# The edge pass of a graph attention layer: own row added ahead of TensorE, bias and sigmoid taken from PSUM

## What is computed

```
for m in range(3):                        # attention
    h = x @ Ws[m]; s = h @ att_src[m]; d = h @ att_dst[m]
    e = leaky(s[src] + d[dst])            # edges and one self loop per node
    w = exp(e - segment_max(e)[dst])
    alpha = w / segment_sum(w, dst)[dst]
    x = x + sigmoid(segment_sum(alpha * h[src], dst) + bias[m])
...                                       # then three message layers of MLP type
```

## Time and profile before

| what | value |
|---|---|
| timed, median of 3 runs | 13333.38 us (13315.89 to 13337.69) |
| profiled execution, its own time | 13224.56 us |
| its span, first to last instruction | 13222.7 us |
| mean granted TensorE clock | 0.73 of full speed |
| edge pass 1 (m = 0) | 2643 to 3433 us, 49 rounds |
| edge pass 2 (m = 1) | 4056 to 4834 us, 49 rounds |
| edge pass 3 (m = 2) | 5465 to 6470 us, 49 rounds |

### The profile page before, as it was taken

The page is one execution under the profiler, slowest core; times in us unless marked ns, Lnnn a source line. Parts: engine busy times, 40 slices in busy tenths (PEclk is TensorE's granted clock), DMA queues, the critical chain, the costliest instruction groups (busy, mean ns, idle before and its releaser), DMA issues.

```text
span 13222.7 us, 165920 instructions
## 1 busy us (share of the span) xinstructions
PE 6805.4 (51%) x35028; PEld 5020.9 (38%) x35028; DVE 5117.0 (39%) x21443; ACT 3990.4 (30%) x8589; POOL 6568.4 (50%) x6253
## 2 busy tenths in 40 slices
PE   6777200077205730355322247777445888444888
PEld 3333100066205630355322235555333555333666
DVE  6777422366315641455322234443112333111444
ACT  7999300033102310233200024443112444111443
POOL 3444566544664566444677743233665333665000
PEclk9999655588657865677555568888556999555999
DMA  6777666644574457533233345565445777444998
GB/s 219 264 262 264 220 237 237 227 126 125 194 261 158 129 174 257 179 119 121 67 45 45 45 117 201 202 202 189 60 58 128 240 234 236 83 58 88 272 268 256
DMA packets 2128228, 2270.53 MB, mean 172 GB/s; under 512 B 234960, under 2 KB 1554869, under 8 KB 2121824
## 3 DMA queue, kind: packets, MB, share of 16 engines
q1 hardware_dynamic: 1798266, 1848.65, 42.2%
q0 software_dynamic: 321440, 418.37, 15.0%
q10 hardware_dynamic: 8390, 2.21, 0.1%
HBM read 1067.73 MB, written 1222.73 MB: 173 GB/s over the span
## 4 chain that ended last, share of the span: by engine, by line
DMA 14%; issue 11%; PE 8%; another core or an unknown queue 5%; POOL 4%; DVE 4%; SPq 3%; POOLq 1%; DVEq 0%; ACT 0%; ACTq 0%
DMA agg_d<-dO,fOI 10%; PE ps L1290 5%; DMA bXd<-agg_d 3%; POOL bO L810 2%; POOL agg_d L801 2%; PE ps L1267 2%; SPq L595 1%; DVE aO L1809 1%; PE ps L1277 1%; DVE bXd L1782 1%; PE ps L1265 1%; SPq L593 1%; DVE eE L1803 1%; SPq L602 0%
## 5 line engine op out<-in xcount | busy, mean ns | idle before, releaser
L862 POOL DMA_INDIRECT bXs<-x_d,fGI x784 | 798.6, 1019 | 1494.8 <-DMA x_d<-aH 1279.9
L801 POOL DMA_INDIRECT agg_d<-dO,fOI x784 | 1212.1, 1546 | 530.9 <-ACT dO L982 296.9
L1290 PE MATMUL ps<-W,aT 128*128 128x128 f32 x9408 | 1206.4, 291 | 22.8 <-ACT aS L999 15.6
L1277 PE MATMUL ps<-aS,W1X 128*128 128x512 f32 x2352 | 1207.4, 594 | 5.4 <-DMA eET<-eaT_d 5.2
L1290 PEld LDWEIGHTS ps<-W,aT 128*128 128x128 f32 x9408 | 1181.7, 208 | 39.7 <-ACT aS L999 25.9
L982 ACT COPY dO<-ps 128x128 f32<-128x128 f32 (+1 forms) x1176 | 318.2, 271 | 2733.7 <-DMA agg_d<-dO,fOI 1526.6
L1817 DVE TENSOR_TENSOR aH<-ps,B 128x512 f32<-128x512 f32 x588 | 406.4, 692 | 1848.1 <-PE ps L1290 1151.8
L1246 PE MATMUL ps<-bO,bNE 128*128 128x128 f32 x1568 | 568.9, 473 | 1021.5 <-ACT dO L982 1010.0
L1005 ACT ACTIVATE aT<-ps,BNT,BNS 128x512 f32<-128x512 f32 x1176 | 882.4, 774 | 609.2 <-PE ps L1278 574.7
L747 POOL DMA_INDIRECT bXs<-x_d,bGI x784 | 784.3, 1000 | 392.8 <-issue 247.7
L1246 PEld LDWEIGHTS ps<-bO,bNE 128*128 128x128 f32 x1568 | 382.5, 305 | 1198.1 <-issue 912.2
(11 more groups left out here) (260 smaller groups left out, 17793.7 us busy)
## 6 DMA issues: line engine op xcount, KB each, us to landing
agg_d<-zeros SPq DMA_DIRECT2D x788, 256.0 KB
bXd<-agg_d SPq DMA_DIRECT2D x784, 256.0 KB
agg_d<-zeros SPq DMA_DIRECT2D x394, 290.0 KB
bXd<-agg_d SPq DMA_DIRECT2D x392, 290.0 KB
x_d<-aO SPq DMA_DIRECT2D x392, 256.0 KB, 2.1
yg_d<-aYG SPq DMA_DIRECT2D x196, 512.0 KB, 3.1
aX<-yg_d SPq DMA_DIRECT2D x392, 256.0 KB, 4.2
x_d<-aH SPq DMA_DIRECT2D x392, 256.0 KB
```

The costliest lines, as they stand in the source:

```text
L801: pool.indirect_dma_start(agg_d[m][u % 2], bass.IndirectOffsetOnAxis(ap=index, axis=0), dO[:, u, 0:AW[m]], None, bounds_check=agg_last, oo ...
L862: pool.indirect_dma_start(fX[:, s, u, 0:C], None, gin_in[m], bass.IndirectOffsetOnAxis(ap=fGI[:, s, u:u + 1], axis=0), bounds_check=n_last ...
L1277: pe.matmul(z, W1X[:, m, h * P:(h + 1) * P], eHT[:, k, :], start=True, stop=False)
L1290: mm = pe.matmul(ps[6 + k][:, j * P:(j + 1) * P], eZ[:, k, h, j * P:(j + 1) * P], W2[:, m, h, :], start=(h == 0), stop=(h == 1))
```

## The change

**Own rows ahead of TensorE.** `diagonals` becomes `own_rows`: ScalarE scales the eight own rows of `pXd` instead of the identity, so it now waits for the loads (`l_in`) and for `p_xw`. A new VectorE step `joined(i+1)` at the end of its round multiplies the source rows by their weight and adds the scaled own rows in place (8 instructions, inputs `bXs` and `bSW`, both in SBUF). AG then has one matmul per tile, not two, and waits for `p_xw`. The masks are the comparison alone.

**Bias row, sigmoid from PSUM.** The denominators are stored to a DRAM tensor `den_d` once per pass and loaded, one row per round, into partition 32 of `pIN`; the bias stands in partition 32 of the carry operand `pCW`. The RW matmul so adds bias times denominator. The 8 VectorE steps L1675 are gone; ScalarE takes 8 sigmoids of one tile each straight from PSUM with 1/denominator as scale, in place of two of four tiles.

**Order.** VectorE does the scan right after the masks and before the dots. ScalarE does the sigmoids of i-1 before the own rows of i+1. The first loads of a pass wait for the end of the softmax section.

```diff
+                sp.wait_ge(z_v, ZV * (m + 1))
+                sp.dma_start(den_d.rearrange("r (h n) -> (r h) n", h=2), slU).then_inc(s_den, 16)
                 load_rows_of(0, 0)
+                sp.wait_ge(s_den, 16 * (m + 1))
...
-                def diagonals(i, s, m=m):
+                def own_rows(i, s, rr, n, m=m):
                     act.wait_ge(p_fe, m * R + i + 1)
+                    act.wait_ge(l_in[s], 32 * (m * RS[s] + n + 1))
+                    if m or past(i - 1):
+                        act.wait_ge(p_xw, m * R + i)
                     for u in range(U):
-                        act.activation(bSW[:, u, :], ident[:, :], ACT.Copy, scale=pFE[:, s, 2, u:u + 1]).then_inc(p_dg, 1)
+                        act.activation(bSW[:, u, :], pXd[:, rr, u, :], ACT.Copy, scale=pFE[:, s, 2, u:u + 1]).then_inc(p_dg, 1)
...
+                    if inside(i - 1):
+                        act.wait_ge(p_fl, r)
+                        if past(i - 2):
+                            act.wait_ge(p_o, 2 * (r - 1))
+                        for u in range(U):
+                            if u % 4 == 0:
+                                act.wait_ge(p_rw, 2 * (r - 1) + u // 4 + 1)
+                            ins = act.activation(bTH[:, u, :], ps[4 + u // 4][:, (u % 4) * P:(u % 4 + 1) * P], ACT.Sigmoid,
+                                                 scale=pFL[:, 1 - s, 1, u:u + 1])
+                            if u % 4 == 3:
+                                ins.then_inc(p_sg, 1)
                     if inside(i + 1):
-                        diagonals(i + 1, 1 - s)
-                    if inside(i - 1):
-                        for g in range(2):
-                            act.wait_ge(p_z, 2 * (r - 1) + g + 1)
-                            act.activation(bTH[:, 4 * g:4 * g + 4, :], bTH[:, 4 * g:4 * g + 4, :], ACT.Sigmoid).then_inc(p_sg, 1)
+                        own_rows(i + 1, 1 - s, (rr + 1) % 4, h + s)
...
                     if inside(i):
-                        pe.wait_ge(l_in[s], 32 * (m * RS[s] + h + 1))
+                        pe.wait_ge(p_xw, r + 1)
+                        pe.wait_ge(p_A, U * (r + 1))
                         for u in range(U):
-                            pe.wait_ge(p_A, U * r + u + 1)
-                            pe.wait_ge(p_dg, U * r + u + 1)
-                            pe.matmul(cols(2 + u // 4, u % 4), bXs[:, s, u, :], pA[s][:, u, :], start=True, stop=False)
-                            mm = pe.matmul(cols(2 + u // 4, u % 4), pXd[:, rr, u, :], bSW[:, u, :], start=False, stop=True)
+                            mm = pe.matmul(cols(2 + u // 4, u % 4), bXs[:, s, u, :], pA[s][:, u, :], start=True, stop=True)
...
+                def joined(i, s, m=m):
+                    for u in range(U):
+                        v.wait_ge(p_dg, U * (m * R + i) + u + 1)
+                        ins = v.scalar_tensor_tensor(out=bXs[:, s, u, :], in0=bXs[:, s, u, :], scalar=pFE[:, s, 1, u:u + 1],
+                                                     in1=bSW[:, u, :], op0=ALU.mult, op1=ALU.add)
+                    ins.then_inc(p_xw, 1)
```

More of the change, by code:

```diff
@@ L81, in gnn_program @@
     ind_d = dram("ind_d", (R, U, U * P))
+    den_d = dram("den_d", (R, U * P))
     gat_src = [xh_d.rearrange("n (t c) -> (n t) c", t=2), x1_d, x2_d]
@@ L539, in p2_round @@
                                      ).then_inc(l_ix[s], 16)
+                        sp.dma_start(pIN[32:33, s, :], den_d[bass.ds(i, 1), :]).then_inc(l_ix[s], 16)
                         if m == M - 1:
@@ L964, in p2_round @@
                             act.copy(pAT[s][:, g * TN:(g + 1) * TN], ps[2 + g][:, :]).then_inc(p_ev, 1)
-                    if inside(i + 1):
-                        diagonals(i + 1, 1 - s)
-                    if inside(i - 1):
-                        for g in range(2):
-                            act.wait_ge(p_z, 2 * (r - 1) + g + 1)
-                            act.activation(bTH[:, 4 * g:4 * g + 4, :], bTH[:, 4 * g:4 * g + 4, :], ACT.Sigmoid).then_inc(p_sg, 1)
-                diagonals(0, 0)
+                    if inside(i - 1):
[9 more added lines that the diff above has]
+                                ins.then_inc(p_sg, 1)
+                    if inside(i + 1):
+                        own_rows(i + 1, 1 - s, (rr + 1) % 4, h + s)
+                if m:
+                    act.wait_ge(p_rw, 2 * m * R)
+                act.copy(pCW[32:33, :], GB[32:33, m, :]).then_inc(p_cb, 1)
+                own_rows(0, 0, 0, 0)
                 p_rounds(act, p2_round)
@@ L1199, in p2_round @@
                         pe.wait_ge(p_ce, r)
-                        pe.wait_ge(l_ix[1 - s], 16 * (m * RS[1 - s] + h + (rr % 2 - 1) // 2 + 1))
+                        pe.wait_ge(l_ix[1 - s], 32 * (m * RS[1 - s] + h + (rr % 2 - 1) // 2 + 1))
                         if past(i - 2):
-                            pe.wait_ge(p_z, 2 * (r - 1))
+                            pe.wait_ge(p_sg, 2 * (r - 1))
                         for u in range(U):
@@ L1216, in _ @@
                 keys_along(1, 1)
+                pe.wait_ge(p_cb, m + 1)
                 p_rounds(pe, p2_round)
@@ L1643, in p2_round @@
                         v.wait_ge(p_dg, U * (r + 1))
+                        v.wait_ge(p_xw, r + 1)
                         v.wait_ge(p_A, U * (r + 1))
@@ L1647, in p2_round @@
                         masks(i + 1, 1 - s)
+                    if inside(i):
+                        if past(i - 2):
+                            v.wait_ge(p_sg, 2 * (r - 1))
+                        v.tensor_copy(pFL[:, s, :, :], keys[:, 4:6, bass.ds(i * U, U)]).then_inc(p_fl, 1)
+                        v.wait_ge(p_ev, 2 * (r + 1))
+                        v.wait_ge(p_fl, r + 1)
+                        if m or past(i - 1):
+                            v.wait_ge(p_c, r)
+                        v.tensor_copy(pC[:, s, 0:1], pC[:, 1 - s, U:U + 1])
+                        scan(pC[:, s, 1:U + 1], pFL[:, s, 0, :], pAT[s][:, P - 1:U * P:P], pC[:, 1 - s, U:U + 1], ALU.mult,
+                             ALU.add).then_inc(p_c, 1)
                     if inside(i - 2) and m < M - 1:
@@ L1659, in p2_round @@
                         v.tensor_copy(SC[:, 1:3, bass.ds((i - 2) * U, U)], bDT[:, 0:2, :]).then_inc(p_dc, 1)
-                    if inside(i):
-                        if past(i - 2):
-                            v.wait_ge(p_z, 2 * (r - 1))
-                        v.tensor_copy(pFL[:, s, :, :], keys[:, 4:6, bass.ds(i * U, U)]).then_inc(p_fl, 1)
-                        v.wait_ge(p_ev, 2 * (r + 1))
-                        v.wait_ge(p_fl, r + 1)
-                        if m or past(i - 1):
-                            v.wait_ge(p_c, r)
-                        v.tensor_copy(pC[:, s, 0:1], pC[:, 1 - s, U:U + 1])
-                        scan(pC[:, s, 1:U + 1], pFL[:, s, 0, :], pAT[s][:, P - 1:U * P:P], pC[:, 1 - s, U:U + 1], ALU.mult,
-                             ALU.add).then_inc(p_c, 1)
-                    if inside(i - 1):
-                        for u in range(U):
-                            if u % 4 == 0:
-                                v.wait_ge(p_rw, 2 * (r - 1) + u // 4 + 1)
-                            ins = v.scalar_tensor_tensor(out=bTH[:, u, :], in0=ps[4 + u // 4][:, (u % 4) * P:(u % 4 + 1) * P],
-                                                         scalar=pFL[:, 1 - s, 1, u:u + 1], in1=GB[:, m, :], op0=ALU.mult,
-                                                         op1=ALU.add)
-                            if u % 4 == 3:
-                                ins.then_inc(p_z, 1)
                     if inside(i - 1):
@@ L1706, in p2_round @@
                             v.tensor_scalar(bNG[:, :], bMV[:, :, 0], -1.0, None, ALU.mult).then_inc(p_mv, 1)
+                    if inside(i + 1):
+                        joined(i + 1, 1 - s)
+                def joined(i, s, m=m):
[4 more added lines that the diff above has]
+                    ins.then_inc(p_xw, 1)
                 for k in range(2):
@@ L1710, in _ @@
                 masks(0, 0)
+                joined(0, 0)
                 p_rounds(v, p2_round)
+                v.wait_ge(s_den, 16 * (m + 1))
                 if m < M - 1:
```

7 lines of the change are left out of this document (4 added, 3 removed).

## The result

The changed kernel takes 13300.8 us (median of 18 runs, 13287.2 to 13317.6), the kernel before 13331.9 on the same chip (18 runs). The ratio is 0.9977, 95% interval 0.9970 to 0.9984: 31 us less, where I forecast 133 less (13200). The sign was right, the size a quarter.

What follows compares the result with a forecast made beforehand. Slowed issue, at about 14 to 15 records a microsecond, was taken to bound passes 1 and 2, the landed-scatter chain pass 3. 157 - 8 - 15 = 134 us less, so 13200 from 13333 us; 8 in 10 range 13040 to 13420.

Steps and rivals of the forecast that it cites:

- The operations and the chain: Passes 1 and 2 after the change: AG, RW, sigmoids, own rows and `joined` sum to 12.3 us a round without slowed issue.
- The rounds of before: Steady mean of the old kernel's rounds: 15.9 us in pass 1 and 15.4 us in pass 2.
- The slowed issue: Passes 1 and 2: issue slowed after bursts, some 4 us in most rounds, read as 14 to 15 records a microsecond.
- I take the rate: Passes 1 and 2: 202 records for 228 give 14.3 and 13.8 us a round, 157 us less in both.
- the slowed issue costs the same 4 us: Rival, 15%: passes 1 and 2 keep the 4 us whatever the instruction count; 16.8 and 16.3 us a round, about 13440 us.
- its formula: With x us of slowed issue kept a round, the change is 49 x (1.75 x - 5.2) + 23 us; slower from 2.7.
- The loop end: Pass 1: VectorE's 6.70 us issue wait once in four rounds stays, about 5.9 us on the longer chain.
- the fourth rival: A loop outgrows what stays loaded, 4%: pass 2 gets the loop-end wait, 66 us lost; pass 1 losing it gains as much.
- Pass 3: Pass 3: scatter chain has none of the changed steps; 0.3 us a round more taken, 15 us in all.
- the third rival: `joined` blocks GpSimd in pass 3, 8%: 2.2 us a round, 108 us; with half the gain elsewhere 13290 to 13370 us.
- Pass starts: First loads of a pass no longer hidden under the softmax section: 2.5 us a pass, 8 us in all.

Runs made afterwards that it cites:

- B: The kernel before the change: 13331.9 us beside the first result, 13230 to 13238 us in later groups, 12324.8 us in one group.
- before_half: B with only every second scatter of a round: 12562.6 us, B there 13231.9; passes 572.4, 501.3 and 719.8 us.
- slim_RW: A with RW's second matmul for each tile (bias row and carried rows) left out: 12392.0 us, B there 12324.8.
- one_dot: A with two of the 16 dot products a round in passes 1 and 2: 13150.6 us, B there 13230.1.
- sig_again: B with only the bias row and sigmoid from PSUM, run again in a later group: 12259.1 us, ratio to B 0.9950.
- A: The kernel after, with the whole change to B: 13300.8 us, ratio to B 0.9977 in the first result.
- double_store: A with the 512 KB of new rows stored a second time each round of passes 1 and 2: 13177.8 us, B there 13230.1.
- early_join: A with own rows ahead of the sigmoids on ScalarE and `joined` ahead of index copy and adds on VectorE: 13196.5 us, ratio to B 0.9964.
- after_again: A run again unchanged in a later group: 12377.5 us, B there 12324.8, ratio 1.0052.
- sig_alone: B with only the bias row in the matmul and the sigmoid from PSUM on ScalarE: 13186.4 us, ratio to B 0.9961.
- late_half: A with every second scatter, in passes 1 and 2 held until the next round's scan: 12878.1 us, B there 13231.9.

## Why the prediction was right and wrong

*The operations and the chain*: right. 12.3 us summed, 11.8 to 12.1 measured where nothing stalls; AG's eight at the lower clock (granted 0.74 to 0.75 over passes 1 and 2, for 0.81 and 0.83); `joined` waits for the own rows 1.7 us in the whole of pass 1, where I allowed 1 us a round. B's 10.38 us too, by before_half. The 12.3 is VectorE's list, and slim_RW bears out that the branch through RW isn't the longer one. Inside that branch two terms were off and cancel: RW starts at the lower level (in the round of 2974.55 its first six matmuls are 0.43 us apart, where I took 0.22 for all), and the sigmoids are 0.27 us apart for the 0.35 that I took.

*The rounds of before*, 15.9 and 15.4 us: too long. From scan to scan they are 15.6 and 14.9. So of the 3.2 us a round that the forecast adds up over both passes, 0.8 weren't there to be had, 39 of the 157 us.

*The slowed issue*, "I take the rate": this step failed. It gave 14.3 and 13.8 us a round, 157 us; the traces show 14.9 and 14.7, 43 us. The number of records sets nothing: the rate went from 12 to 21 a us in these kernels (one_dot, sig_again). What the runs show in its place is a hold-up beside GpSimd's indirect transfers, in four groups of the experiments' five: halving the scatters takes it away. Its cost isn't fixed: B loses 4.5 us a round to it in pass 2 (14.9 to 10.4), A 2.6 (14.7 to 12.1). So a chain 1.7 us longer cost nothing and 0.2 us was gained. The rival "the slowed issue costs the same 4 us" came nearer. It had the right remark, that the chain has grown and nothing hides that once issue isn't the limit; in the group without the stall the change is slower. And it said that from 2.7 us kept the change loses: with 2.6 for x its formula gives 9 us less, from the same too long rounds of before. That the sign came out right is in good part luck: 2.6 is only 0.1 us below that bound, and the loop end, which was to stay, gave most of the rest.

*The loop end*: predicted to stay at 5.9 us once in four rounds. It vanished (68.9 to 9.6 us of issue). I had this as the fourth rival's other half, "if pass 1 loses it", 66 us; under the stall it was worth about 21. That is half of what was gained in the two passes: pass 1 got 32 us, pass 2, which never had the wait, 11. Together -43.5 us, against the forecast's -157.

*Pass 3*: 15 us more forecast, 24.5 measured in A's profile on the first chip, 19 in double_store, about 10 without the stall. The chain is the forecast one, with the landed scatter in it. By its parts, the mean of 41 rounds: from index copy to the end of the statistics 5.19 us in B and 5.59 in A; through GpSimd's three operations to the first scatter 3.37 and 3.52; the eight scatters 10.18 in both; landing 1.66 and 1.64. So two parts have grown. In the second, the third rival is true in small. `joined` beside GpSimd's power operation, first B, then A:

```profile
L785 POOL TENSOR_TENSOR bRS<-bRS,mhalf x47: 1667/1671/1677, 5466.4 to 6398.5; 128x8 f32<-128x8 f32 x47
```

```profile
L791 POOL TENSOR_TENSOR bRS<-bRS,mhalf x47: 1810/1814/1877, 5459.6 to 6415.9; 128x8 f32<-128x8 f32 x47
```

0.14 us a round, 7 us; in early_join, where `joined` lies elsewhere, it is 1671 again. The Trainium skill (SBUF — State Buffer, Who interferes with whom) calls the port pair that VectorE and GpSimd share an exclusive lock. The rows show contention, but no instruction held for the whole of the other: GpSimd's is 0.14 us longer, and no step of `joined` in this pass takes over 354 ns. The other part, 0.40 us a round, is the stall again. I had the sigmoids "done some 2 to 4 us ahead of the index copy's release"; ScalarE in pass 3 (index copy at 5677.09):

```profile
5672.72 1.14 ACT L981 ACTIVATE bTH<-ps,pFL 128x128 f32<-128x128 f32 x4 [3.90 <-PE ps L1223]
5677.01 1.14 ACT L981 ACTIVATE bTH<-ps,pFL 128x128 f32<-128x128 f32 x4 [3.15 <-remote]
```

The first four are; the other four are held and delay the second add. In after_again the first part is back at 5.20 us and the second stays at 3.52.

*Pass starts*, 8 us: not resolved. The stretch from the last scan of pass 1 to the first of pass 2 is 664 to 676 us in B alone, 679 in A and 664 in sig_alone, which starts its passes like A.

Left open: what holds the engines, and why one group is free of it; that TensorE's keys or RW take part in it is only argued, since the two runs meant for it met the group without the stall, and the gather pass is held without them. late_half shows that the place of the scatters matters. Why the loop end went isn't shown. A ratio of A in the other groups with the stall wasn't measured. Of the kernels that compute the whole result, sig_alone, the bias row and sigmoid from PSUM alone, has the lowest ratio to B in both conditions, 0.9961 (level with early_join's 0.9964) and 0.9950.

## What to carry to other kernels

Before pricing a shared limit ("issue slowed", "so many records a us"), halve the one thing that runs beside it and see what the loop's own chain is: four scatters instead of eight gave the chain that a group without the stall showed later, to 0.3 us. Work moved from a branch into a loop's only chain costs its full length as soon as the stall that covers it is gone, so a gain measured under a stall lasts no longer than the stall does. Of a change with several parts, run each part alone: here one part held all the gain (0.4 to 0.5%), another lost 0.6% alone, and their sum was not the whole. And look at a stretch that the change doesn't touch before you name the engines that a stall needs: here VectorE was held in the gather pass too.

## What was not expected of the hardware

- ScalarE starts 2.4 us behind the end of the RW that it waits for (L981 at 2965.93, RW over at 2963.5), in the median 1.3 to 1.5 us, beside GpSimd's scatters of 0.98 us; with half the scatters 0.04 us, and 11.9 for 14.9 us a round.
- VectorE is held by "issue" for 254 to 270 of 900 us between its own dots beside GpSimd's gathers, with TensorE and ScalarE idle; in one group of runs not at all.
- The same kernel takes 13332, 13230 or 12325 us in different groups of runs, the last two under the same chip number, and the ratio of the same two kernels is 0.9977 or 1.0052.
- Scatters whose rows are all dropped but row 0 stall nearly as much as those that write (14.6 and 14.2 us a round).
- A loop end of 6.7 us "issue" can go away through an edit of the loop's body (68.9 to 9.6 us a pass), but not through a mere change of order (67.8).
